# Moving the scores ahead of the remainder products in each attention step

## The reference

```python
q = layernorm(x) @ Wq;  k = ctx @ Wk;  v = ctx @ Wv      # 16 heads of 64
probs = softmax(q @ k.T / 8)
x = x + tanh(g_xattn) * ((probs @ v) @ Wo + bo)
y = layernorm(x)
out = x + tanh(g_ffn) * moe(y)    # top 2 of 8 experts, fc1 -> relu -> fc2
```

## Time and profile before

| | |
|---|---|
| median of 3 runs | 997.7 us (997.68 to 999.24) |
| the profiled execution, its own time | 997.99 us |
| its span in the trace | 996.3 us |
| PE busy | 954.7 us, 96% |
| DVE, ACT, POOL busy | 676.6, 506.1, 282.0 us |
| mean granted clock of TensorE | 0.985 of full |
| attention, steps 0 to 63 | to about 570 us of the span |

### The profile page before, as it was taken

One profiled execution on the slowest core, in us unless ns is written; L12 is line 12 of the kernel. 1 busy time (PEld: TensorE's weight loads), 2 busy tenths in 40 slices (PEclk: granted clock), 3 DMA queues, 4 the chain that ended last, 5 costly groups with the idle time before them and its releaser, 6 DMA issues.

```text
span 996.3 us, 18970 instructions
## 1 busy us (share of the span) xinstructions
PE 954.7 (96%) x7192; PEld 833.6 (84%) x7192; DVE 676.6 (68%) x1542; ACT 506.1 (51%) x1566; POOL 282.0 (28%) x293
## 2 busy tenths in 40 slices
PE   7799999999999999999999888999999999999996
PEld 5587887888878878878888787999999999999995
DVE  4768677787786886886776862757575665657572
ACT  3567466564663773674664621535354343435351
POOL 6703025025033042052041033222222223232222
PEclk8989999999999999999999989999999999999998
DMA  9096003011020030021011015353442435352521
GB/s 258 21 301 190 22 2 107 23 43 65 23 80 29 22 96 33 2 86 44 1 44 44 7 57 161 83 126 91 85 127 49 127 48 129 50 129 60 143 48 22
DMA packets 63098, 76.62 MB, mean 77 GB/s; under 512 B 6033, under 2 KB 55096, under 8 KB 63008
## 3 DMA queue, kind: packets, MB, share of 16 engines
q1 hardware_dynamic: 50720, 59.18, 19.8%
q0 software_dynamic: 12288, 16.23, 9.0%
HBM read 46.52 MB, written 29.49 MB: 76 GB/s over the span
## 4 chain that ended last, share of the span: by engine, by line
PE 79%; ACT 7%; DVE 6%; POOL 3%; DMA 2%; issue 2%; SPq 1%; POOLq 0%; DVEq 0%; another core or an unknown queue 0%
PE down L1202 6%; PE down L1201 6%; PE down L1200 6%; PE up L1186 6%; PE up L1187 6%; PE up L1188 6%; PE score L541 5%; PE out_bank L529 5%; PE probT L516 5%; ACT probs_odd L726 3%; ACT work L726 2%; PE query_bank L462 2%; PE query_bank L460 2%; PE query_bank L461 2%; PE key_bank L485 2%; PE rT L1170 2%
## 5 line engine op out<-in xcount | busy, mean ns | idle before, releaser
L1142 POOL DMA_INDIRECT out_dram<-eo,index x64 | 99.5, 1554 | 281.6 <-ACT eo L1244 249.3
L1236 ACT ACTIVATE hid<-up,b 128x512 f32<-128x512 f32 x128 | 88.3, 690 | 84.4 <-PE up L1188 84.4
L726 ACT ACTIVATE work<-score,negmax 128x128 f32<-128x128 f32 x256 | 91.4, 383 | 42.1 <-DVE negmax L903 41.1
L726 ACT ACTIVATE probs_odd<-score,negmax 128x128 f32<-128x128 f32 x256 | 91.3, 382 | 41.8 <-DVE negmax L903 41.2
L403 POOL DMA_INDIRECT disp<-packed,slots x64 | 68.2, 1066 | 133.5 <-DVE slots L894 94.2
L691 ACT ACTIVATE k_sb<-key_bank 128x512 f32<-128x512 f32 x64 | 38.8, 606 | 126.5 <-PE key_bank L485 126.2
L903 DVE TENSOR_REDUCE negmax<-score 128x4 f32<-128x512 f32 x128 | 81.9, 682 | 20.5 <-PE score L541 20.1
L1244 ACT ACTIVATE eo<-eo_raw,gate 128x256 f32<-128x256 f32 x64 | 30.9, 506 | 122.4 <-DVE eo_raw L1306 122.4
L1297 DVE TENSOR_TENSOR hid_l<-hid,hid_h 128x512 fp32r<-128x512 f32 x128 | 88.6, 693 | 4.4
L911 DVE COPY pT<-probT 128x512 f32<-128x512 f32 x128 | 82.0, 682 | 9.1 <-PE probT L516 9.0
L1306 DVE TENSOR_TENSOR eo_raw<-down,b 128x256 f32<-128x256 f32 x64 | 25.8, 423 | 86.4 <-PE down L1202 86.4
(11 more groups left out here) (250 smaller groups left out, 2804.0 us busy)
## 6 DMA issues: line engine op xcount, KB each, us to landing
rows<-disp SPq DMA_DIRECT2D x18, 516.0 KB, 5.2
w_raw<-fc1T_dram SPq DMA_DIRECT2D x9, 1024.0 KB, 8.3
w_raw<-fc_dram SPq DMA_DIRECT2D x9, 1024.0 KB, 11.3
disp<-fixed SPq DMA_DIRECT2D x1, 8256.0 KB, 33.5
rows<-x_dram SPq DMA_DIRECT2D x16, 512.0 KB
out_dram<-rows SPq DMA_DIRECT2D x8, 512.0 KB, 2.9
c_raw<-ctxT_dram SPq DMA_DIRECT2D x8, 256.0 KB
c_raw<-ctxT_dram SPq DMA_DIRECT2D x16, 128.0 KB
```

The lines of the kernel that those rows point to most:

```text
L726: last = nc.scalar.activation(probs[w % 2][:, c, :], score[hh][:, b * P:(b + 1) * P], ACT.Exp, bias=negmax[:, w % 2, c:c + 1], accum_out=s ...
L1142: pool.indirect_dma_start(out=out_rows[:, :], out_offset=bass.IndirectOffsetOnAxis(ap=index[half][:, i:i + 1], axis=0), in_=eo[half][:, i, ...
L1236: nc.scalar.activation(hid[m % 2][:, :], up[m % 2][:, :], ACT.Relu, bias=b1[par][:, m:m + 1]).then_inc(s_hid, 1)
```

## The change

In each step the call of `scores(u)` moves ahead of the two remainders. Before: main products, side work, remainders, scores, weighted sums. After: main products, side work, scores, remainders, weighted sums. Nothing is added or removed, and the orders of the other engines stay as they are.

```diff
             if kinds[1:]:
                 pe.wait_ge(s_at_split, w)
                 misc(kinds[1], out_bank, u // NP)
+            scores(u)
             if u + 1 < STEPS:
                 keys_rest(u + 1)
             if i < STEPS:
                 values_rest(value_bank, i)
-            scores(u)
             if w >= 0:
                 if kinds[1:]:
                     pe.wait_ge(*misc_done(kinds[1], u // NP))
```

## The result

The changed kernel took 1003.62 us (median of 6 runs, 1001.62 to 1005.98) against 998.52 us for the kernel before, measured beside it (6 runs, 997.68 to 999.24): ratio 1.0055, 95% interval 1.0043 to 1.0068. That is slower, and above my range. The profiled execution took 1003.16 us with a span of 1001.4, at a mean granted clock of 0.984 (before: 996.3 and 0.985), so the clock is no part of it.

A forecast was written before the change was run, and what follows sets the result against it. PE's order was taken to bound the kernel, other engines mattering only where PE waits. Terms -0.5 + 0.66 + 0.10 + 0.45 + 0.84 - 0.3 gave +1.25 us: 999.0 against 997.7, range 996.0 to 1002.5.

The forecast's parts named there:

- ACT behind the scores: ACT's copies k_sb and v_sb now precede the exponentials, 2.41 us behind the scores; next q_sb not late for PE, cost 0.
- the absorption of j = 0: PE's spare wait before the output projection takes up the 0.22 us in groups 3, 5, 6; 0.10 may remain in group 2.
- j = 0: Steps waiting for q_sb: remainders lose their cover, weighted sums 0.22 us later; +0.66 us in groups 1, 4, 7.
- The seams: PE, scores to remainders 0.99 plus remainders to weighted sums 0.32: 1.31 against 1.33 us; -0.5 us over some 46 steps.
- Rival A: PE's new seam shows a weight load (0.11 us) or drains the array (0.20 in all): 1005 to 1010 us; chance 7%.
- j = 3: Scores would have to wait for q_sb, 0.13 us less 0.01 lost per step, in 7 groups: +0.84 us.
- Step 3: Group 0's wait for q_sb, at the lower clock: the 0.22 us loss becomes +0.45 us.
- The end: Steps 62 and 63: scores no longer share their start with K's remainder and finish earlier, -0.3 us.
- rival C: Late maxima in j = 0 and 1 come at once, holes before the projection close: 995.5 to 997 us; chance 12%.
- rival B: ACT becomes late, with k_sb and v_sb between scores and exponentials; waits grow: 1001.5 us, slower; chance 27%.
- the split's later release: POOL's split of the context waits for K's last remainder, some 1 us later, six times: cost 0.
- D: No change at all: losses in j = 0 and 3 are taken up by later waits, 997.7 us; chance 15%.

The follow-up runs named there:

- j6: Kernel before with the scores moved ahead of the remainders only in steps with j = 6: 992.41 us, ratio 0.9982 to the kernel before.
- new_again: The changed kernel, unchanged, measured and traced again in a later comparison with the kernel before: 995.17 us, ratio 1.0008.

## Why the prediction was wrong

The step that failed is "ACT behind the scores: cost 0", and with it the absorption of j = 0 that rested on it. In the first comparison PE's signals came up to 1.3 us late in j = 0 and 1, k_sb with them, and the stretches where this happened hold 4.2 of the 5.2 us. The seams and the losses of j = 0 and 3 came as reckoned, and a gain in j = 6 was missing from the sum. Term by term:

**The seams: right.** 0.91 and 0.41 in place of 0.99 and 0.32, the sum 1.33 for my 1.31. The remainders' load does hide behind the scores: were it to show, scores to remainders would be 0.91 + 0.11 = 1.02. Rival A fell: it asked for 0.11 more at least. The Trainium skill's rule in TensorE: Matmul & The Clock Gate, "The mechanism", that weight loads overlap matmuls in flight only when the row group differs, would have shown the load, and the trace disagrees at the new seam as at the old. The -0.5 from the seams didn't come, as 1.33 is what the old order had.

**j = 0: the size right, the absorption wrong.** +0.24 per group against +0.22, in every trace of the changed order. The step "the 0.22 are absorbed, if q_sb comes when it does now" failed: the condition didn't hold. In the first comparison q_sb came later, and the stops before the projection grew from 1.7 to 2.8 us. On the later chips there were no such stops to absorb anything (0.00 to 0.11 us of idle time before each projection).

**j = 3: right**, +0.12 to +0.13 for +0.12. **Step 3**: +0.43 from scores to weighted sums (2.44 against 2.01) for +0.45, but the granted clock was back at 2.4 GHz at 53.74 instead of 54.80, and the next queries start 4.83 behind the scores instead of 5.21, so the loss was taken back. **The end**: -0.14 for -0.3.

**ACT behind the scores: the step that failed.** "Cost 0" rested on k_sb 1.42 behind the scores, and this holds wherever PE's signal comes at once. I had seen in the earlier trace rows that a start behind PE can be 0.9 late in j = 0 and 1, and used it only for rival C, as something that might go away. I should have asked what the change moves into that stretch: K's remainder and k_sb. Once there, k_sb is late in eleven steps, with the maximum or one step later, v_sb and the exponentials queue behind it on ACT, and this is rival B's mechanism at twice its price: +2.5 us between j = 0 and 1 and +1.7 instead of -0.8 before the projection. These two cells are 4.2 of the 5.2 us; 0.43 of it stands in step 9, where no signal is late. That they are tied to late signals is read from the traces; that nothing else makes them is supported by the three later pairs, where the late signals are absent and both cells are gone: there j = 0 to 1 costs 0.01 to 0.02 per group, and no stop stands before the projection. B's number (1001.5) was nearer than my own, but its sign misled: the exponentials of j = 5 do start 2.75 behind their scores, beyond its bound of 2.6, in the first trace and in the later ones alike, and the interval to j = 6 grew by 0.01 at most. Two readings of the prediction are off by the trace: the nine late maxima are eight, and the exponentials of j = 7 stood 3.57 behind their scores already, not 2.4 to 2.8.

**The gain in j = 6: not foreseen.** I had looked at the split's later release and called it free; it is worth 1.7 us, because it leaves DVE's additions alone. The run j6 shows it by itself, and the size follows the additions' time group by group.

**What belongs to the change.** In the three later pairs, each on one chip, the ratio of the changed kernel to the kernel before is 1.0008, 0.9985 and 1.0010, and no interval reaches beyond 0.25%. The steps j = 0 and 3 (some +2.5 with the 0.02 of j = 0 to 1) and j = 6 (-1.7) with the end nearly cancel (+0.6 left), the pace of the projection gives up to 0.4 per group back, and single executions differ by some 2 us up to step 8 and by 4 us up to step 16. The 0.55% of the first comparison was seen only together with the late signals. Of the rivals this is D in its size, though not in its reason. What C hoped for, late maxima gone and no stop before the projection, is there on the later chips, but in both orders, so the change doesn't bring it.

**What stays open.** Why PE's signals are late in the first comparison's two traces and in none of the 18 later ones, where none is more than 0.14 behind its matmul up to step 63. In j = 0 they come 0.74 to 0.85 behind POOL's fourth indirect transfer, but that is a coincidence in time, not a cause shown: in step 24 of new_again the same transfer stands at the same place, 0.34 to 1.31 behind the scores' start, and nothing is late. Nor is it shown that the chip makes them: the record names the chip of every later run, but not that of the first comparison. And the recording itself is a rival that no run tests: the first two traces hold 551 and 527 of the 1024 raisings by which the indirect transfers report that they have landed, the later ones with all transfers 1014 to 1023.

## What to carry to other kernels

A late start whose reason the trace doesn't show belongs in the forecast as a cost for whatever the change moves next to it, not only as a gain that might appear. When an order on one engine is changed, look at which side work of the others is released by the moved instruction and what it then runs beside: here that was the only gain. And a difference of half a per cent should be measured again, on other chips, before it is explained: the same two kernels gave 1.0055 in one comparison and 0.9985 to 1.0010 in three others.

## What the runs showed of the hardware

- ACT started k_sb 0.02 us behind the raising of the semaphore that it waits for, late or not. In the first two traces these raisings came up to 1.06 (scores) and 1.30 us (K's remainder) behind the end of their matmul, in j = 0 and 1 of groups 2 to 7, while PE worked on; in the 18 later traces no signal of PE up to step 63 came more than 0.14 behind.
- DVE's four additions took 0.80 us alone and 1.47 to 1.64 beside POOL's split; its divisions 0.69 alone and 0.95 to 1.76 beside it.
- 256-column fp32r matmuls started every 0.1136 or 0.1178 us at the same granted clock, a pace kept through all 96 of a group. In traces without late signals, from step 18 on, the slow one stands in all 66 projections of kernels without the new order in both j = 0 and 1, and the fast one in 39 of the 42 with it.
- From the remainders (64 rows) to the next product with 128 rows it took 0.41, against 0.32 from the last 128-row product of 512 columns to the remainders.
